# Four graph layers on one core: cell groups two places later in the first product, and four smaller moves

## The reference, cut to what matters

```python
# layer 0 (gate): gnn_out = x1 = h @ W1 + b1, then four times
norm  = dis[row] * dis[col]                # dis = max(degree, 1) ** -0.5
alpha = tanh(x_i @ gw[:512] + x_j @ gw[512:] + gb)
gnn_out = gnn_out + segment_sum(norm * alpha * x_j, col)
x = x + concat([x1, gnn_out])
# layer 1: W is 1024 x 1024, W.at[src, dst].add(edge_weight); x = x + h @ W.T + bias
# layer 2: x = x + relu(segment_sum(dinv[src] * dinv[dst] * (h @ W)[src], dst) + b), with self loops
# layer 3 (attention): e = exp(-leaky_relu(al[src] + ar[dst])); h' = segment_sum(e * h[dst], src) / rowsum
#          x = x + elu(h')
```

## Time and profile before

| | |
|---|---|
| median of 3 runs | 1001.96 us |
| the profiled execution: its own time / its span | 1001.58 us / 1000.0 us |
| TensorE busy | 977.4 us (98%) |
| VectorE, ScalarE, GpSimd busy | 668.7, 430.9, 140.4 us |
| granted TensorE clock, mean | 0.999 |

### The profile page before, as it was taken

One profiled execution on the slowest core, in us unless ns is written; L12 is line 12 of the kernel. 1 busy time (PEld: TensorE's weight loads), 2 busy tenths in 40 slices (PEclk: granted clock), 3 DMA queues, 4 the chain that ended last, 5 costly groups with the idle time before them and its releaser, 6 DMA issues.

```text
span 1000.0 us, 14720 instructions
## 1 busy us (share of the span) xinstructions
PE 977.4 (98%) x5170; PEld 809.6 (81%) x5170; DVE 668.7 (67%) x1221; ACT 430.9 (43%) x650; POOL 140.4 (14%) x191
## 2 busy tenths in 40 slices
PE   5999999999999999999999999999999999999997
PEld 3788788888888888888888888888888888888886
DVE  7877888788778879354485343216446664988886
ACT  5688865554543646112242322233222232445543
POOL 3022500000000010232221000000110000333331
PEclk9999999999999999999999999999999999999999
DMA  7256580000000014745433111243451230101223
GB/s 251 101 177 222 136 255 1 1 22 0 0 21 0 0 12 104 178 171 188 180 124 116 42 42 43 77 155 106 156 180 69 69 121 0 43 22 64 84 84 122
DMA packets 27326, 93.42 MB, mean 93 GB/s; under 512 B 3530, under 2 KB 3530, under 8 KB 27136
## 3 DMA queue, kind: packets, MB, share of 16 engines
q1 hardware_dynamic: 16400, 58.07, 16.5%
q0 software_dynamic: 10880, 34.74, 11.4%
HBM read 64.48 MB, written 33.56 MB: 98 GB/s over the span
## 4 chain that ended last, share of the span: by engine, by line
PE 91%; DVE 5%; ACT 2%; issue 1%; POOL 1%; DMA 0%; ACTq 0%; DVEq 0%; POOLq 0%
PE ps L592 32%; PE ps L2052 11%; PE ps L1972 9%; PE ps L1974 9%; PE ps L1973 9%; PE ps L2025 5%; PE ps L2024 5%; PE ps L575 3%; PE ps L1895 1%; PE ps L1897 1%; PE ps L1896 1%; PE ps L1866 1%; PE ps L1822 1%; PE ps L1825 1%; PE ps L1838 1%
## 5 line engine op out<-in xcount | busy, mean ns | idle before, releaser
L1972 PE MATMUL ps<-g_hi,mask_hi 128*128 128x512 f32 x400 | 157.4, 394 | 2.1 <-DVE mask_lo L1513 2.1
L1974 PE MATMUL ps<-g_hi,mask_lo 128*128 128x512 f32 x400 | 155.9, 390 | 0.0
L1973 PE MATMUL ps<-g_lo,mask_hi 128*128 128x512 f32 x400 | 155.7, 389 | 0.0
L558 ACT ACTIVATE hT_hi<-ps 128x1024 fp32r<-128x1024 f32 x40 | 41.0, 1025 | 200.3 <-PE ps L575 200.3
L592 PE MATMUL ps<-w_hi,hT_hi 128*128 128x512 f32 x320 | 126.4, 395 | 0.0
L592 PE MATMUL ps<-w_lo,hT_hi 128*128 128x512 f32 x320 | 124.7, 390 | 0.0
L2052 PE MATMUL ps<-y_all,att_hi 128*128 128x512 f32 x400 | 110.0, 393 | 1.5 <-DVE att_lo L1693 1.5
L1110 ACT ACTIVATE mask<-ps,v 128x640 f32<-128x640 f32 x80 | 63.4, 793 | 111.2 <-PE ps L1974 52.9
L592 PE MATMUL ps<-w_hi,hT_lo 128*128 128x512 f32 x320 | 98.6, 389 | 0.0
L1972 PEld LDWEIGHTS ps<-g_hi,mask_hi 128*128 128x128 f32 x400 | 75.1, 188 | 20.4 <-DVE mask_lo L1513 3.3
L2052 PEld LDWEIGHTS ps<-y_all,att_hi 128*128 128x128 f32 x400 | 74.0, 188 | 17.3 <-DVE att_lo L1693 1.5
(11 more groups left out here) (203 smaller groups left out, 1839.2 us busy)
## 6 DMA issues: line engine op xcount, KB each, us to landing
xin<-x_after SPq DMA_DIRECT2D x30, 512.0 KB, 3.3
xres<-x_after POOLq DMA_DIRECT2D x20, 512.0 KB, 4.2
x_after<-xres POOLq DMA_DIRECT2D x20, 512.0 KB, 3.0
w_raw<-in_L_gnn_W SPq DMA_DIRECT2D x8, 1024.0 KB, 7.2
x_after<-g POOLq DMA_DIRECT2D x20, 256.0 KB, 7.4
xres<-x_after SPq DMA_DIRECT2D x10, 512.0 KB, 3.4
xin<-in_x SPq DMA_DIRECT2D x9, 512.0 KB, 3.4
out_x<-xres SPq DMA_DIRECT2D x9, 512.0 KB, 2.7
```

Source lines behind the costliest of these rows:

```text
L1972: nc.tensor.matmul(SUMS[dd], mask_hi[k][:, cols], g_hi[:, s, :], start=(s == 0), stop=False)
L1973: nc.tensor.matmul(SUMS[dd], mask_hi[k][:, cols], g_lo[:, s, :], start=False, stop=False)
L1974: last = nc.tensor.matmul(SUMS[dd], mask_lo[k][:, cols], g_hi[:, s, :], start=False, stop=(s == T - 1))
```

## The change

There are five edits.

1. SHIFT = 2 is subtracted in `groups_at` and `tiles_behind`, so every group of cells and all transposes behind it come two places (half a tile) later on all three engines. The last group moves from tile 8, place 0 to tile 8, place 2, and the last count rows to tile 9, place 0. DVE's gates 2 to 5 are respread behind them, and ACT's `place_act(9, 0)` stands behind `take_x1(8)`. SCALES_AHEAD is adapted: factors 1 and 2 ahead of the stores of tile 0, factor 3 ahead of tile 3, factor 4 ahead of tile 7.
2. On POOL the five operations on edge weights stand ahead of `scale_pool(0)`. On ACT the bias of tile 0 stands behind six copies of W1's high part and no longer behind two.
3. ACT loads the square root table at the end of tile 8. The line that loaded the tanh table early is gone.
4. `mask_hi_of(0, 0)` stands ahead of the second tanh.
5. In the last pair, DVE's two `elu_end` stand behind the last `att_rest`, and ACT waits for them (`gat_added`) before it overwrites `gat_sums`.

```diff
+SHIFT = 2
-SCALES_AHEAD = {0: 1, 1: 2, 4: 3, 7: 4}
+SCALES_AHEAD = {0: (1, 2), 3: (3,), 7: (4,)}
@@ groups_at, tiles_behind
-        g = PER_STEP * (t - FIRST_STEP) + place + lead
+        g = PER_STEP * (t - FIRST_STEP) + place - SHIFT + lead
-        g = PER_STEP * (t - FIRST_STEP) + place - behind
+        g = PER_STEP * (t - FIRST_STEP) + place - SHIFT - behind
@@ gpsimd
-        pool.wait_ge(firsts_done, 1)
-        scale_pool(pool, 0)
         pool.wait_ge(ew_landed, 16)
...
         nc.gpsimd.tensor_copy(part[2], left_over[1]).then_inc(parts_chain, 1)
+        pool.wait_ge(firsts_done, 1)
+        scale_pool(pool, 0)
@@ scalar
-            if k == 2:
+            if k == 6:
                 place_bias(0)
...
-            place_act(t, 0)
+            if t < T - 1:
+                place_act(t, 0)
             if t > 0:
                 take_x1(t - 1)
+            if t == T - 1:
+                place_act(t, 0)
...
             place_act(t, 3)
+            if t == T - 2:
+                nc.scalar.activation(rden[:, 0, 1:2], zeros[:, 0:1], ACT.Sqrt).then_inc(tanh_idle, 1)
...
-        nc.scalar.activation(rden[:, 0, 0:1], zeros[:, 0:1], ACT.Tanh).then_inc(tanh_idle, 1)
...
+        mask_hi_of(0, 0)
         tanh(0, 0, 0, 1)
-        mask_hi_of(0, 0)
...
+        act.wait_ge(gat_added, T - GRP - 1)
         gat_take(T - 2, 0)
         elu_act(T - 2, 0)
+        act.wait_ge(gat_added, T - GRP)
@@ vector, attention_dve
-                if not first and s in (7, 8):
+                if not first and not last and s in (7, 8):
                     elu_end(GRP * (grp - 1) + s - 7, grp - 1, s - 7)
+            if last:
+                for j in range(GRP):
+                    elu_end(GRP * (grp - 1) + j, grp - 1, j)
```

More of the change, by code:

```diff
@@ L852, in _ @@
         nc.gpsimd.tensor_copy(part[2], left_over[1]).then_inc(parts_chain, 1)
+        pool.wait_ge(firsts_done, 1)
+        scale_pool(pool, 0)
         for a in range(T):
-            if a in SCALES_AHEAD:
-                scale_pool(pool, SCALES_AHEAD[a])
+            for i in SCALES_AHEAD.get(a, ()):
+                scale_pool(pool, i)
             pool.wait_ge(count_row_ready, a + 1)
@@ L1417, in _ @@
             place_dve(t, 1)
-            if t == T - 2:
-                gates(3, 3)
             if t + 2 < T:
@@ L1437, in _ @@
             if t == T - 2:
+                gates(3, 3)
+            place_dve(t, 2)
+            if t == T - 2:
                 gates(4, 4)
-            place_dve(t, 2)
             place_dve(t, 3)
+            if t == T - 2:
+                gates(5, 5)
             if t == T - 3:
@@ L1569, in half_dve @@
                     g_rest(s - HT, T * nxt + s - HT)
-        gates(5, 5)
         dve.wait_ge(counts_copied, CELL_GROUPS)
```

## The result

The changed kernel took 1005.45 us (median of 9 runs, 1003.20 to 1006.62), the kernel before 1002.14 us in the runs beside it. The ratio is 1.0028, interval 1.0018 to 1.0037: **slower by 2.8 us**. (The two medians by themselves lie 3.3 us apart; the ratio on record is not their quotient. The ratios are used from here on.) The prediction was 1002.8 us with a range up to 1004.8; the result lies outside.

A forecast was written before the change was run, and what follows sets the result against it. TensorE, busy 977.4 of 1000.0 us, was taken as the bound, so only its waits count. Terms -0.7 - 0.3 - 0.7 + 2.4 + 0.1 + 0.4 = +1.2 on 1001.58 gave 1002.8 us, range 998.6 to 1004.8.

The forecast's parts named there:

- Part 1: Start, weights' parts first on POOL: TensorE's wait falls from 2.5 to 0.7 us, gain 0.7 us (0.1 to 2.4).
- Nothing else covers this: Start, closing claim on putting the weights' parts first: nothing else covers its gain of 0.7 us.
- 2(a): Start, groups two places later: the 1.7 us wait at the fourth group becomes about 1.4, gain 0.3 us (0 to 0.7).
- (b): Tile 4, groups two places later: the 0.7 us wait is covered by a weight row's transposes, gain 0.7 us.
- 2(c): Tiles 7 and 8: late factor 4 makes group 22 wait 1.1 to 1.5 us; loss 2.4 us (0.3 to 2.8).
- Part 3: Before the gates, square root table and mask order: cover shrinks by two places, 0 to 0.3 us lost, 0.1 taken.
- Part 4: End, last elu ends: 1.12 us wait goes but the residual's transfer comes later, loss 0.4 us (gain 1.1 to loss 1.0).
- B: Slower rival: late factor 0 eats the start's gain whole, +3.1 us, 1004.7 us; chance 0.2.
- A: Faster rival: POOL is in time at both places, at the start and at tiles 7 and 8, 998.5 us; chance 0.25.
- C: Rival for the whole kernel: nothing shows, each wait is only renamed, 1001.6 us; chance 0.15.

The follow-up runs named there:

- Edit 1 with factor 4 early: Kernel before with edit 1 alone, but factor 4 ahead of the stores of node tile 6: 1000.11 us, ratio 0.9982.

## Why the prediction was wrong, step by step

- **Part 1, gain 0.7: a loss of 0.8 us (1.5 in the changed kernel itself, 1.1 give or take 0.7 in the fit). This is the step that failed.** Its rows came within their bounds: parts at 13.7, `bias_scale` ready at 17.28, subtractions at 20.0, tile 2 at 32.16. Wrong was "Nothing else covers this": I read the gain at TensorE's tile 2, and did not see that the wait at the second group then grows by most of what tile 2 wins (1.6 for 0.3). My own sum had the relu of tile 3, on which that wait hangs, end at 32.6 and so later than its 31.89 before. What counted was DVE's chain to the statistics of tile 4, and DVE starts that chain behind the subtractions that wait for the late bias. The traces show why the gain is missing and, through the slow cast, a loss of 0.4 to 0.5 us in the mean, less than their scatter; the rest of the loss stands in the medians alone, and its cause is open. That a cast could be shut out for 4 us I did not have; the Trainium skill (SBUF — State Buffer, on the shared port pair) speaks of one whole instruction, which would have made 1.1 us of it (an estimate: 0.39 + 0.7). Here the measurement decides. The sign was in the earlier trace rows: I called the cast of 2.00 us a case of that rule, but it is 1.6 us over its equal, more than one subtraction of 0.71.
- **2(a) and (b), gain 1.0: the mechanism was right and the size was off.** Edit 1 with factor 4 early wins 1.8 us. I left 1.4 us of the wait at (a) standing; by itself edit 1 takes it to 0.3, and it is edit 2 that brings 1.6 back. The two steps were not independent.
- **2(c), loss 2.4: right, 2.6 to 2.7 measured**, but not from the parts I added. The wait was 1.44 (I had 1.1 to 1.5), the count row 0.5 (0.6). With the clock at 1.00 the first gate sum comes 2.0 us later by it. In the changed kernel the falling clock, 1.4 us in about half of the executions, would bring the rest; it was in none of my terms. In edit 1 alone it did not fall, and there the rest is within the noise.
- **Part 3, loss 0.1: 0.7 for the order of masks, nothing for the table.** I gave edit 4 no price, as a swap of two operations. By the traces the first gate sum gains about 0.1 by it, and the way from there loses 0.7.
- **Part 4, loss 0.4: 0.3 (0.8 in the changed kernel).** Right: the transfer ends last.
- **The sum** was -0.7 - 1.0 + 2.4 + 0.1 + 0.4 = +1.2. Measured terms: +0.8 - 1.8 + 2.6 + 0.9 + 0.3 = +2.8, where the 0.9 are the 0.7 of edit 4 and the 0.2 left over. That this is the measured ratio proves nothing: the terms are steps from the kernel before to the changed one, and add up to it by the way they are taken. Of the 1.6 us between the sums, part 1 makes 1.5 and part 3 0.8, and the larger gain of edit 1 takes 0.8 back. The profiled execution (+1.6) had a quick cast and a full clock, so it alone looked like a hit.
- **Rivals.** B had the right side and nearly the size, by a factor 0 that eats the start. Its condition, the bias of tile 0 at 18.4 or later, was met in two of eight profiles (factor ready at 18.7 and 18.8), through the cast and not the factor's own operations; in a third with a slow cast the factor was ready at 17.98. The rest of B's loss came from elsewhere, so its nearness in size is in part luck. A and C fell.

What stays open: whether edit 2 costs 0.5 us or 1.5, why the cast is caught in some executions and for how long, and why the wait of 1.4 us lets the clock fall in some executions only.

## What to carry to other kernels

Follow a gain past the engine that waits to the one that sets the next wait. If two terms of a sum speak of the same stretch, work them out together: taking away a wait may only name it anew a few microseconds on. When a whole schedule is shifted, look at each helper task placed by a table (here one factor, ahead of or behind two stores): with edit 1 alone this one number decided between 1000.1 and 1002.3 us. And a swap of two operations in front of a loop that runs at its slowest engine's pace costs what it delays that engine, not what it does to the first result.

## What the runs showed of the hardware

- A POOL cast of 80x250 that began within 0.2 us of the start of a row of six DVE subtractions (0.1 and 0.2 ahead, 0.1 behind) took 4.04, 4.13 and 2.65 us; it took 0.73 to 0.76 when begun 0.16 to 0.49 us into the row, and 0.39 with DVE held back. In the kernels with the start of before, a POOL operation on 80x250 begun from 0.5 us ahead of DVE's subtractions to 0.1 behind their start took 1.6 to 2.0 us in five of six profiles. Small operations (128x2) begun within the row of six took 0.5 to 1.2 us each.
- Behind a wait of 1.4 us and one of 0.45 TensorE's granted clock went to 0.50 for some 3 us in one profile and stayed at 1.00 in others; behind 2.2 us, and behind 2.5 us in another place, it fell in the profile too. Behind the 2.5 us for `ew_part` in the kernel before it stayed at 1.00 (stretch from 0 to 20 us).
